# Four units in each pass of every loop instead of two, in a three-stage Perceiver block

## The reference

```
x = x + cross_attention(layernorm(x), ctx, ctx, mask)   # 16 heads of 32, 512 keys
x = x + self_attention(layernorm(x))                    # 16 heads, 64 keys, biases
x = x + ffn(layernorm(x))                               # 512 -> 2048 -> 512, relu
```

## Time and profile before

| | before |
|---|---|
| runs | 1743.09, 1744.25, 1746.99 us |
| span of the profiled execution | 1745.7 us (the page has no other time for it) |
| TensorE busy | 1689.3 us, 97% |
| VectorE, ScalarE, GpSimd busy | 1032.7, 701.8, 216.0 us |
| instruction queues | 101 packets with 1.65 MB; 23 packets with 0.19 MB |
| granted TensorE clock | 0.993 on average |

### The profile page before, as it was taken

One profiled execution on the slowest core, in us unless ns is written; L12 is line 12 of the kernel. 1 busy time (PEld: TensorE's weight loads), 2 busy tenths in 40 slices (PEclk: granted clock), 3 DMA queues, 4 the chain that ended last, 5 costly groups with the idle time before them and its releaser, 6 DMA issues.

```text
span 1745.7 us, 38877 instructions
## 1 busy us (share of the span) xinstructions
PE 1689.3 (97%) x16268; PEld 1416.7 (81%) x16268; DVE 1032.7 (59%) x1492; ACT 701.8 (40%) x1689; POOL 216.0 (12%) x300
## 2 busy tenths in 40 slices
PE   6899999999999999998999999999899999999999
PEld 4688878788878788787888898989688888888887
DVE  3655556555565555667677777776674445544543
ACT  2555555665555566566422222323222222222221
POOL 1000000000000000122111121211032012202200
PEclk9999999999999999999999999999999999999999
DMA  6011111111111111333010101001101101100000
GB/s 218 13 62 62 62 62 61 52 59 62 61 62 55 48 54 54 132 132 139 26 49 24 48 24 41 31 27 57 51 31 49 49 1 49 48 17 31 25 24 24
DMA packets 48668, 95.00 MB, mean 54 GB/s; under 512 B 5792, under 2 KB 14112, under 8 KB 47264
## 3 DMA queue, kind: packets, MB, share of 16 engines
q1 hardware_dynamic: 48544, 93.16, 15.7%
HBM read 67.97 MB, written 25.17 MB: 53 GB/s over the span
## 4 chain that ended last, share of the span: by engine, by line
PE 90%; DVE 6%; issue 2%; ACT 2%; DMA 0%; DVEq 0%; SPq 0%; ACTq 0%
PE project L339 49%; PE project L1273 13%; PE scores L685 4%; PE scores L1791 3%; PE probs_t_psum L1791 3%; PE scores L1789 3%; PE probs_t_psum L1789 3%; PE probs_t_psum L694 3%; PE attended_t L711 2%; PE probs_t_psum L1379 2%; PE scores L491 1%; PE attended_t L1398 1%; DVE ff_weight_scratch L1224 1%; PE attended_t L1252 1%; DVE w_ternary L1227 1%
## 5 line engine op out<-in xcount | busy, mean ns | idle before, releaser
L1273 PE MATMUL project<-ff_xt,w_ternary 128*128 128x512 f32 x1024 | 256.4, 393 | 0.0
L1273 PEld LDWEIGHTS project<-ff_xt,w_ternary 128*128 128x128 f32 x1024 | 190.0, 188 | 38.4
L1282 ACT ACTIVATE hidden<-project,b_sb 128x512 f32<-128x512 f32 x128 | 88.2, 689 | 326.1 <-PE project L1273 326.1
L887 ACT ACTIVATE cross_scores_probs<-cross_scores_probs,exp_bias,logit_scale 128x128 f32<-128x128 f32 x256 | 122.6, 482 | 97.9 <-DVE exp_bias L1033 97.9
L339 PE MATMUL project<-self_xt_hi,self_w_hi 128*128 128x256 f32 x512 | 148.4, 290 | 3.2 <-DVE self_xt_lo L502 2.3
L339 PE MATMUL project<-self_xt_lo,self_w_hi 128*128 128x256 f32 x512 | 145.1, 283 | 0.0
L339 PE MATMUL project<-self_xt_hi,self_w_lo 128*128 128x256 f32 x512 | 145.0, 283 | 0.0
L887 ACT ACTIVATE cross_probs<-cross_scores,exp_bias,logit_scale 128x128 f32<-128x128 f32 x256 | 122.8, 483 | 0.4 <-DVE exp_bias L1033 0.4
L339 PE MATMUL project<-ctx_hi,cross_w_hi 128*128 128x512 f32 x256 | 107.0, 418 | 15.2 <-DVE ctx_lo L1052 15.2
L339 PE MATMUL project<-cross_w_hi,ctx_hi 128*128 128x512 f32 x256 | 108.8, 425 | 0.0
L339 PEld LDWEIGHTS project<-self_xt_hi,self_w_hi 128*128 128x128 f32 x512 | 98.4, 192 | 6.3 <-DVE self_xt_lo L502 2.6
(11 more groups left out here) (175 smaller groups left out, 4098.5 us busy)
## 6 DMA issues: line engine op xcount, KB each, us to landing
ctx_raw<-in_ctx SPq DMA_DIRECT2D x64, 256.0 KB, 4.0
cross_xt_raw<-in_x_t SPq DMA_DIRECT2D x64, 128.0 KB, 2.2
cross_x<-in_x SPq DMA_DIRECT2D x32, 256.0 KB, 3.0
x<-cross_x SPq DMA_DIRECT2D x32, 256.0 KB, 2.0
self_x<-x SPq DMA_DIRECT2D x32, 256.0 KB, 2.8
ff_w_raw<-in_w SPq DMA_DIRECT2D x2, 4096.0 KB, 13.8
x<-self_residual SPq DMA_DIRECT2D x32, 256.0 KB, 2.0
ff_x<-x SPq DMA_DIRECT2D x32, 256.0 KB, 3.4
```

The lines of the kernel that those rows point to most:

```text
L887: last = nc.scalar.activation(c_p[buf][:, cols], c_s[buf][:, cols], ACT.Exp, bias=exp_bias[:, buf, g:g + 1], scale=logit_scale[:, parity(u ...
L1273: last = nc.tensor.matmul(PJ[m % 2][:], w1_q[:, c, cols], x_t[parity(v)][:, c, :], start=(c == 0 and x_t is fxt_hi), stop=(c == DC - 1 and ...
L1282: nc.scalar.activation(h_raw[:, m % 2, :], PJ[m % 2][:], ACT.Relu, bias=b1_sb[:, m:m + 1]).then_inc(h_relu, 1)
```

## The change

The loop of `run_steps` now does four units in one pass. The counter `turn` starts at 0, and `turn * 2 + 1` takes the place of `half`; the four units of a pass have `off` 0 to 3. The units' numbers, their order, the instructions of each and the values that they wait for stay as they were. The cross and self stages have three passes instead of six, the feed-forward stage one instead of two. The change holds for all five engines and for both versions of the cross stage.

```diff
--- before.py
+++ after.py
@@ -110,9 +110,9 @@
 
     step(Unit(0, 0), "full")
     step(Unit(0, 1), "full")
-    with eng.Fori(1, units // 2 - 1) as half:
-        step(Unit(half, 0), "full")
-        step(Unit(half, 1), "full")
+    with eng.Fori(0, (units // 2 - 2) // 2) as turn:
+        for off in range(4):
+            step(Unit(turn * 2 + 1, off), "full")
     step(Unit(units // 2 - 1, 0), "last_but_one")
     step(Unit(units // 2 - 1, 1), "last")
```

## The result

The changed kernel took 1751.47 us (median of six runs, 1748.28 to 1753.42) against 1744.03 us of the kernel before, measured beside it: ratio 1.0036, 95% interval 1.0024 to 1.0048. It is slower, by 7.4 us between the medians and 6.3 us by the ratio. The forecast was 1743.8 us and no change that a measurement could tell. The profiled execution took 1749.4 us, with a span of 1747.6 us, so 1.8 us lie around the span.

The account below looks back on a forecast made before the run. TensorE, busy 97% of 1745.7 us, was taken as the bound. Cross -3.0 and self +2.5, all else 0, gave 1745.2 us on the profiled execution; off the median 1744.25, 1743.8 us, range 1740.8 to 1747.0.

Parts of the forecast that it names:

- its two jumps: Self stage, before units 6 and 10: five free jumps become two that miss, 1.25 us net each, +2.5 us.
- Feed-forward: Feed-forward stage: the one jump between its two passes goes; it costs nothing today, so 0.
- the other engines: Loops of ScalarE, VectorE, SyncE and GpSimd double too; any miss fits into existing waits, so 0.
- code that is fetched straight on: Inside a cross pass: code fetched on the way causes no pause; units stay 44.84 us apart.
- The limit between 1698 and 1824 records: TensorE's instruction store: the self loop of 1698 records stays, the cross loop of 1824 doesn't; the limit lies between.
- The two that stay jump over twice the code, which is already refetched today, so their price stays.: Cross stage, jumps before units 6 and 10: each keeps today's price of 0.99 us.
- The cross term: Cross stage: three of five jumps back go, at 0.99 us each, -3.0 us.
- The uncovered jump: Rival, self stage, before scores of units 6 and 10: uncovered misses cost 2.5 us each, total 1746.3 us; chance 0.2.
- their cover: Self stage, before scores: six queued pairs keep TensorE working for 0.98 us of the fetch, leaving scores 1.48 us late.

Follow-up runs that it names:

- straight cross loop: Kernel before, but TensorE's cross loop does its twelve units in one pass and never jumps back: 1741.32 us against 1745.29, ratio 0.9977.

## Why the prediction was wrong

*What held.* A jump back to code that is gone costs, and the self loop of four units is gone: its two jumps were put at 1.25 us each and cost 1.1 and 1.2. Feed-forward cost nothing (the changed kernel is 1.9 us behind at its start and at its end), nor did the other engines (1.0006, interval 0.9996 to 1.0016) or code that is fetched straight on. The limit between 1698 and 1824 records was read as one of size, which it isn't; it changed no term here. The same reading of the packets led to the straight cross loop, for which 5.0 us were expected and 4.0 came.

*"The two that stay jump over twice the code, which is already refetched today, so their price stays."* This step failed. A jump's price was taken as a constant of the jump, 0.99 us, since five of them agreed. They agreed because it was one and the same jump; the two that stayed cost 2.5 and 2.4 us in the changed kernel, and 1.0 and 0.5 when only its place was moved by 128 instructions. A body of another length puts the end elsewhere in its block: 228 instructions behind a border before, 44 behind one after. The reading that fits the table and the two packets in one stall, and which no run proves, is that the sequencer has then just asked for the next straight block, which nobody will use, when it asks for the target; the packets carry no address, so which block each one holds isn't shown. The Trainium skill (Runtime: NRT & Kernel Launch, section Instruction fetch mechanics) has two sentences that bear on this: prefetch goes only straight on, and kernels do better fully unrolled. The packets here don't contradict the first. The straight cross loop, 4.0 us faster, agrees with the second; the self loop, no faster straight (1741.54 against 1741.32 us), shows that it holds only for a loop that doesn't stay in the engine. The cross term was -3.0 us; measured it is -0.1 in stalls (two of 2.5 and 2.4 against 4.97), and +1.5 with one drop.

*The granted clock was no term of the sum.* Jumps with no stall above 1.6 us had no drop behind them in any profile. In each of the four profiles with this place of the cross loop (two of the changed kernel, one with the cross stage alone, one with TensorE's loops alone) one of the two stalls had one and the other had not: drops stand behind 2.47, 2.17, 2.62 and 1.87 us, none behind 2.31, 2.15, 1.95 and 2.11 us. So the length doesn't decide it. That the stalls come first and the drops right behind them is shown; what makes the one and not the other drop is not.

*Which rival came near.* The uncovered jump had the direction and came nearest with 1746.3 us, still 5.2 too low, but its mechanism isn't what happened. The self jumps had their cover, and the cross jumps had the same matmuls ahead of them as before; what grew was the fetch. In the profiled pair 1.5 + 2.1 us of the jumps give +3.6, and the -1.7 us in the rest of that pair go with the 3.4 us less of half clock there. The step from there to the 7.4 us between the medians rests on the clock of the single runs, whose traces aren't there: how many more drops the longer runs have, and at which jump, stays open.

## What to carry to other kernels

Before changing the size of a loop, look at the instruction queue in the DMA view, pass by pass: no packets means that the body stays in the engine, and growing it, or only moving it, can end that. Where a body doesn't stay anyway, make the loop longer until no jump back is left on the engine that bounds the kernel; code that is fetched straight on was free here, and that saved 4.0 us of 1745. Stopping half-way, with fewer but worse placed jumps, made this kernel slower. A price read from one jump holds for the place of that jump in the code; in another place it was up to six times as much.

## What the runs showed of the hardware

72 idle instructions of TensorE, none of them on the critical path, made a kernel of 1745 us 61 us slower. Every change of TensorE's program that stands ahead of a loop moves its ends, so a comparison of two kernels with such a loop carries an uncertainty of several microseconds that has nothing to do with what was changed: here 1747.5, 1751, 1757 and 1762 us for the same work with 32, 0, 64 and 128 idle instructions, of which only the 128 took time of their own, about 4 us.

A loop of 1729 instructions stayed with TensorE in one place and did not when it was moved by 72 instructions. By the borders reckoned above it touched seven blocks of 256 in the first place and eight in the second. In the run with the cross stage alone changed, its start lies 238 instructions ahead of a border, where it again touches seven, and it stayed: no packet in 905 to 1204 us. No loop of another size tested this limit.
